# Causal attention with sixteen heads: one column-tile stretch a pair of steps, maxima at the front of each score stretch, the diagonal mask added by TensorE

## What is computed

```python
scores = jnp.einsum('bhqd,bhkd->bhqk', q, k) / math.sqrt(dk)
causal = jnp.tril(jnp.ones((S, S), dtype=bool))
scores = jnp.where(causal[None, None], scores, -jnp.inf)
attn = jax.nn.softmax(scores, axis=-1)
ctx = jnp.einsum('bhqk,bhkd->bhqd', attn, v)
```

## Time and profile before

| | |
|---|---|
| Median of 3 runs | 1840.8 us (1836.97 to 1855.38) |
| Span of the profiled execution | 1836.8 us |
| PE busy | 1737.2 us, 95% of the span |
| DVE busy | 1167.2 us, 64% |
| POOL busy | 804.4 us, 44% |
| ACT busy | 784.3 us, 43% |
| PE weight loads busy | 1010.7 us, 55% |

### The profile page before, as it was taken

How to read it: one execution, slowest core, us unless ns; L and a number is a source line. 1 busy time by engine, 2 the same in 40 slices (tenths; PEclk the granted TensorE clock), 3 DMA queues, 4 the chain that set the end, 5 groups by cost and what they waited for, 6 DMA issues and landing times. The chain is left out here.

```text
span 1836.8 us, 33962 instructions
## 1 busy us (share of the span) xinstructions
PE 1737.2 (95%) x9952; PEld 1010.7 (55%) x9952; DVE 1167.2 (64%) x2630; ACT 784.3 (43%) x1544; POOL 804.4 (44%) x434
## 2 busy tenths in 40 slices
PE   6999995789999999989999998999999996999998
PEld 5888884444444444444445444444444433677776
DVE  6667663687767767657767775776776704566564
ACT  3222221135555545545555554554555563222321
POOL 1333333335655646535655564564664672111211
PEclk9999998599999989989999998999999997999999
DMA  5556545830161161142115006116102003131221
GB/s 172 201 197 220 194 166 174 185 72 24 25 139 25 25 131 33 25 90 70 30 35 124 25 10 137 25 25 135 29 25 71 12 7 101 41 134 69 83 100 47
DMA packets 103259, 157.60 MB, mean 86 GB/s; under 512 B 10544, under 2 KB 43824, under 8 KB 100400
## 3 DMA queue, kind: packets, MB, share of 16 engines
q1 hardware_dynamic: 93296, 136.10, 27.4%
q10 hardware_dynamic: 9792, 19.40, 2.9%
HBM read 96.23 MB, written 58.72 MB: 84 GB/s over the span
## 5 line engine op out<-in xcount | busy, mean ns | idle before, releaser
L771 ACT ACTIVATE a_probs<-a_st 128x512 f32<-128x512 f32 (+3 forms) x1280 | 613.2, 536 | 543.3 <-PE a_st L661 277.7
L618 POOL TENSOR_TENSOR a_pair<-a_probs 128x1024 f32<-128x1024 f32 (+2 forms) x320 | 614.8, 1938 | 396.7 <-ACT a_probs L771 396.7
L790 DVE TENSOR_REDUCE a_part<-a_mx 128x1 f32<-128x512 f32 x768 | 507.7, 684 | 208.8 <-PE a_mx L649 206.8
L649 PE MATMUL a_mx<-a_k_stack,a_q_stack 96*128 96x512 f32 (+3 forms) x1280 | 493.5, 428 | 45.1 <-DMA a_q_stack<-qk_scratch 24.5
L661 PE MATMUL a_st<-a_q_stack,a_k_stack 98*128 98x512 f32 (+3 forms) x1280 | 447.9, 393 | 5.1 <-ACT a_probs L771 2.2
L649 PEld LDWEIGHTS a_mx<-a_k_stack,a_q_stack 96*128 96x128 f32 x1280 | 229.7, 196 | 389.5 <-DVE a_part L790 179.5
L794 DVE CUSTOM_DVE_ANT_0 a_mx<-a_mx,a_mask 128x384 f32<-128x384 f32 (+3 forms) x512 | 250.5, 498 | 140.7 <-PE a_mx L649 138.1
L661 PEld LDWEIGHTS a_st<-a_q_stack,a_k_stack 98*128 98x128 f32 x1280 | 242.8, 193 | 83.6 <-ACT a_probs L771 52.7
L217 POOL TENSOR_TENSOR p_rot<-p_mul 128x1024 f32<-128x1024 f32 x32 | 90.7, 2836 | 213.3 <-DVE p_mul L412 213.3
L675 PE MATMUL a_av<-a_probs,shared 128*32 128x512 f32 (+3 forms) x1280 | 161.7, 551 | 0.7
L675 PE MATMUL a_av<-a_probs,a_v 128*32 128x512 f32 (+3 forms) x1280 | 160.0, 546 | 0.7
(11 more groups left out here) (138 smaller groups left out, 1656.8 us busy)
## 6 DMA issues: line engine op xcount, KB each, us to landing
a_q_stack<-qk_scratch SPq DMA_DIRECT2D x96, 256.0 KB, 4.9
a_k_stack<-qk_scratch SPq DMA_DIRECT2D x21, 1024.0 KB, 13.7
qk_scratch<-p_rot_hi SPq DMA_DIRECT2D x32, 512.0 KB, 3.1
qk_scratch<-p_rot_lo SPq DMA_DIRECT2D x32, 512.0 KB, 3.9
v_scratch<-p_v_st SPq DMA_DIRECT2D x32, 256.0 KB, 6.1
ctx_scratch<-a_ctx_st SPq DMA_DIRECT2D x32, 256.0 KB, 2.4
f_ctx<-ctx_scratch SPq DMA_DIRECT2D x8, 1024.0 KB, 8.9
f_x<-in_x SPq DMA_DIRECT2D x8, 1024.0 KB, 7.8
```

What stands on the lines that cost most here:

```text
L618: pool.tensor_tensor(pair[:, p % 2, h:h + 2, q0:TT], probs[:, s % RING, h:h + 2, q0:TT], probs[:, (s + 1) % RING, h:h + 2, q0:TT], ALU.add ...
L649: pe.matmul(mx_ps[k % BANKS][:, 0:width], q_stack[0:96, t, h, qi * P:(qi + 1) * P], k_stack[par][0:96, h, c * TT:c * TT + width], start=Tr ...
L771: act.activation(probs[:, s % RING, h, q0:TT], st_ps[:, (HG * s + h) % BANKS, q0:TT], ACT.Exp, scale=SCORE_SCALE).then_inc(exp_done, 1)
L790: dve.tensor_reduce(out, mx_ps[k % BANKS][:, :], AX.X, ALU.max).then_inc(max_done, 1)
```

## The change

It does five things.

1. Work goes by pairs of steps. PE issues the eight score products of the next pair, then one column stretch that holds the values of both steps and the sums of the same pair (`values_and_sums`). ACT waits for the sums once a pair, and the ring `a_probs` has four steps.
2. The items of a pair stand among its eight scores, two ahead of the first and then about one ahead of each, none in the column stretch. The table now counts by pairs, and the counts differ by up to two from those of the two steps before.
3. On the diagonal an item gets its mask on PE: a second, bf16 product of `a_later` and `a_eye` of 128 columns into the same bank. DVE then takes a `tensor_reduce` for every item, of the item's width. The mask in SBUF, its memset and its wait go.
4. On DVE `turn_sums` stands ahead of the items of a pair, `invert` and `turn_back` behind the first and the second; `unit_max` still comes behind the items of the stretch in which a unit's items end.
5. SP's waits and the order of its copies follow the pairs.

```diff
-LAG = 2
-RING = 5
+RING = 4
+LAST_PAIR = [e // 2 for e in UNIT_END]
...
-PER_FIRST = 7
+PER_FIRST = 14
...
+    room = [width(2 * p + 2) + width(2 * p + 3) + 2 * width(2 * p) + width(2 * p + 1) + 0.5 for p in range(NPAIR)]
+    for e in LAST_PAIR:
+        room[(e + 1) % NPAIR] -= 1.0
...
-                pe.matmul(mx_ps[k % BANKS][:, 0:width], q_stack[0:96, t, h, qi * P:(qi + 1) * P],
-                          k_stack[par][0:96, h, c * TT:c * TT + width], start=True, stop=True).then_inc(item_done, 1)
+                mm = pe.matmul(mx_ps[k % BANKS][:, 0:width], q_stack[0:96, t, h, qi * P:(qi + 1) * P],
+                               k_stack[par][0:96, h, c * TT:c * TT + width], start=True, stop=c < t)
+                if c == t:
+                    mm = pe.matmul(mx_ps[k % BANKS][:, width - P:width], later[:, :], eye[:, :], start=False, stop=True)
+                mm.then_inc(item_done, 1)
...
+            def values_and_sums(g, par, p):
...
+                pe.wait_ge(exp_done, exps(g, steps[1], HG - 1))
+                if unit_first:
+                    pe.wait_ge(av_copied, 4 * g + t + START)
+                for n, (s, q) in enumerate(zip(steps, (q0, q1))):
+                    for h in range(HG):
+                        mm = pe.matmul(av_ps[h * DK:(h + 1) * DK, q:TT], vb[par][:, j + n, h * DK:(h + 1) * DK],
+                                       probs[:, s % RING, h, q:TT], start=unit_first and n == 0,
+                                       stop=unit_last and n == 1, tile_position=(0, h * DK))
+                mm.then_inc(values_done, 1)
...
+                pe.wait_ge(pair_added, 2 * (NPAIR * g + p) + 2)
+                for h in range(HG):
+                    mm = pe.matmul(sum_ps[h * DK:(h + 1) * DK, q1:TT], ones[:, :], pair[:, p % 2, h, q1:TT],
+                                   start=unit_first and q1 == q0, stop=unit_last, tile_position=(0, h * DK))
+                mm.then_inc(pair_done, 1)
...
+                for p in range(NPAIR):
+                    items = [(n, k) for n, k in items_of_pair(p, first) if not (n and last)]
                     issued = 0
+                    for i in range(2 * HG):
+                        while issued < len(items) and issued * 2 * HG <= (i + 1) * len(items):
...
+                    values_and_sums(g, par, p)
...
-                    wait_alone(dve, item_done, NITEM * g + k + 1, dve_passed)
-                    dve.tensor_tensor_reduce(out=mx_ps[k % BANKS][:, 0:width], in0=mx_ps[k % BANKS][:, 0:width],
-                                             in1=mask[:, TT - width:TT], scale=1.0, scalar=3.0 * MASKED,
-                                             op0=ALU.add, op1=ALU.max, accum_out=out).then_inc(max_done, 1)
+                width = TT if c < t else (qi + 1) * P
+                dve.wait_ge(item_done, NITEM * g + k + 1)
+                dve.tensor_reduce(part[:, h * SUB + qi, c:c + 1], mx_ps[k % BANKS][:, 0:width], AX.X,
+                                  ALU.max).then_inc(max_done, 1)
```

More of the change, by code:

```diff
@@ L77, in plan_items, with items_before, items_of_pair, units_ended_at_pair @@
 def plan_items():
[L80 to L84, removed]
+    room = [width(2 * p + 2) + width(2 * p + 3) + 2 * width(2 * p) + width(2 * p + 1) + 0.5 for p in range(NPAIR)]
+    for e in LAST_PAIR:
+        room[(e + 1) % NPAIR] -= 1.0
+    done = [sum(room[:p]) / sum(room) * NITEM for p in range(NPAIR + 1)]
     return [HEAD_START + round(d) for d in done]
 PLAN = plan_items()
[L91 to L110, removed]
+def items_before(p, first):
+    steady = PLAN[p % NPAIR] + NITEM * (p // NPAIR)
+    return min(BEFORE_FIRST + PER_FIRST * p, steady) if first else steady
+def items_of_pair(p, first):
+    return [(f // NITEM, f % NITEM) for f in range(items_before(p, first), items_before(p + 1, first))]
+def units_ended_at_pair(p, first):
+    return [(n, ITEMS[k][0]) for n, k in items_of_pair(p, first) if k in ITEM_END]
+def unit_ended_before(p, pairs):
+    e = p - pairs
+    return [(int(e < 0), t) for t in range(QT) if LAST_PAIR[t] == e % NPAIR]
 def wait_alone(eng, semaphore, value, passed):
@@ L619, in add_pairs @@
                                            probs[:, (s + 1) % RING, h:h + 2, q0:TT], ALU.add).then_inc(pair_added, 1)
-                    for ahead, t_out in unit_ended_before(s, 1):
-                        if not (ahead and first):
-                            divide(g - ahead, t_out)
+                    for before, t_out in unit_ended_before(p, 1):
+                        if not (before and first):
+                            divide(g - before, t_out)
             def divide(g, t):
@@ L700, in sums @@
                 mm.then_inc(pair_done, 1)
             def group(g, par, use, next_use, first, last):
-                for s in range(NSTEP):
-                    items = [(n, k) for n, k in items_of_step(s, first) if not (n and last)]
+                for p in range(NPAIR):
+                    items = [(n, k) for n, k in items_of_pair(p, first) if not (n and last)]
                     issued = 0
-                    add_pair = (s - LAG) % 2 == 1 and not (s < LAG and first)
-                    total = width(s + 1) + width(s) + (width(s - LAG) if add_pair else 0.0)
-                    def items_due(work):
-                        nonlocal issued
-                        while issued < len(items) and issued * total <= work * len(items) + 1e-6:
+                    for i in range(2 * HG):
+                        while issued < len(items) and issued * 2 * HG <= (i + 1) * len(items):
@@ L858, in _ @@
             group(GROUPS - 1, False, True)
-            for part_of, _, _ in PARTS:
-                part_of(GROUPS - 1, QT - 1)
+            turn_sums(GROUPS - 1, QT - 1)
+            invert(GROUPS - 1, QT - 1)
+            turn_back(GROUPS - 1, QT - 1)
 class Early:
```

164 lines of the change are left out of this document (62 added, 102 removed).

## The result

The changed kernel takes 1895.5 us (median of 4 runs, 1892.0 to 1896.5), the kernel before 1838.9 us (4 runs, 1832.3 to 1855.4). The ratio is 1.029, with a 95% interval from 1.024 to 1.034: 57 us slower. The forecast was 1930, 34 us too high. The direction was right, and so was the cause of most of the loss; the sum's +96 us was 39 too large. The profiled execution has a span of 1894.2 us.

A forecast was written before the change was run, and what follows sets the result against it. The prediction took PE to bound the attention (busy 1147 of 1172 us). Switches, masks and bursts (-15), loop turn (+4), unit_max meeting POOL (+72) and clock (+35) gave +96 on 1836.8: 1933, stated as 1930 us, range 1830 to 1975.

The forecast's parts named there:

- The switches: PE between array products and column stretches: 0.343 us lost per stretch, 320 stretches fewer, -110 us.
- The mask products: Diagonal items on PE: 512 second products at 0.125 us each, +64 us; 20 us if every weight load hid.
- The bursts: Items among scores wait for DVE behind three banks: 5.6 us a group after the change, little of the 110 left.
- its -15: Sum over all groups of switches, mask products and bank waits on PE: -15 us.
- The hand rules: Products of a group's 20 pairs timed by predecessor or bank release: 139.5 us a group before, 137.2 after.
- unit_max and POOL: CAST and subtraction behind pairs 1, 9, 11, 15 held by POOL's additions: 10.1 us a loop group, +72 us.
- the 1 us named: Sign of being right: CAST and subtraction behind pairs 1, 11 and 15 last 1 to 2.4 us each.
- The clock: Half clock on PE behind 14 waits of about 4 us, 2.5 us each: +35 us, from 0 to 70.
- That unit_max slips by: Rival: the CAST precedes POOL at pairs 1 and 11, or both instructions run beside POOL: 1826 us; chance 0.23.
- That the subtraction gets in between POOL's two instructions: Rival: only the CAST is held, DVE is free 2.3 us sooner: 1864 us; chance 0.10.
- The third: Rival: the clock falls for 10 us behind each long wait, 35 becomes 70: 1975 us; chance 0.09.
- The loop turn: At DVE's loop end PE's wait grows from 1.21 to 1.9 us, six times: +4 us.

The follow-up runs named there:

- e9: Kernel before with unit_max's three tensor_reduces (as in e3) and VectorE reducing only the last 128 columns of each item: 1822.3 us.
- e12: e7 without the 512 mask products of the items: 1710.1 us.
- e5: e1 with the mask of the diagonal items added by VectorE again instead of by a product on PE: 1796.7 us.
- e7: e1 with VectorE reducing only the last 128 columns of each item, all of PE's work kept: 1747.3 us.
- e3: Kernel before with unit_max's CAST and subtraction replaced by three small tensor_reduces of one SBUF input each: 1832.0 us.
- e1: Changed kernel with unit_max's CAST and subtraction replaced by three small tensor_reduces of one SBUF input each: 1802.3 us.
- e2_one_of_two: Changed kernel with only unit_max's CAST replaced by a tensor_reduce, the subtraction kept: 1843.1 us.

## Why the prediction was right, and where it was off

The runs part both kernels into the same layers. The columns add up by construction. Each entry but the first line's is the difference of two runs that differ in one thing; e9 and e12 differ in the whole order of work, stretches, places of the items and turn alike. The order in which layers are taken off matters too, as e5 showed for the masks.

| us | before | after | change | predicted |
|---|---|---|---|---|
| PE's own work with ACT's pace, items without mask products | 1822.3 (e9) | 1710.1 (e12) | -112 | -110 |
| mask products on PE | 0 | 37.1 (e7 - e12) | +37 | +64 |
| DVE's pace behind three banks | 9.7 (e3 - e9) | 55.0 (e1 - e7) | +45 | +31 |
| unit_max beside POOL, with the clock | 7.5 (before - e3) | 93.2 (after - e1) | +86 | +107 |
| loop turn of DVE | | | in the rows above | +4 |
| sum | 1839.5 | 1895.4 | +56 | +96 |

**The forecast.** The working gives +96, which is 1937 us on the median before of 1840.8. It was added to a span of 1836.8 instead, taken for an execution 4 us below the median, and 1933 was then rounded down; but in the runs here a time is 1.7 to 3.9 us longer than its span, so a short span says little. By this the stated time came out nearer than the working.

**The switches: right in price, and by luck so close in the sum.** Three losses of 0.095, 0.143 and 0.105 us were read from single rows, and 320 of them came to 112 us instead of 110. One stretch more cost 0.25 to 0.37 us in a pair at PE's pace. But the working had the same gain in every group, 13.7 us, and between e9 and e12 (by first exponentials) it is 16 to 18 in the groups of the loop without a loop end of PE, 10 in the first and 4 in the last. In the last, a pair without items even grew from 5.93 to 6.29 us. The very pair from which the price was read gained nothing, since ACT set its length afterwards.

**The mask products: mis-sized, the largest single miss.** The step "512 items get one: +64 us" took the price of a 512 wide product for all. It should have been kept as one end of a range: measured 37 us, and 42 in the order of before.

**The bursts: mechanism right, 14 us too small in the sum.** The prediction found that much of the gain from the switches vanishes behind the banks. Its 5.6 us for a group of the loop was met: 5.5 between e7 and e1. The +31 of the table is what its -15 leaves beside -110 and +64, and it has 1.7 us a group taken off for ACT's holds before, 14 us over eight groups, which the table's first line contains; no run separates them. Without the meeting with POOL the change is 30 us better than before (e1 against e3), not 11 (-15 and the loop's +4); the masks' 27 us too much and the bursts' 14 too little leave most of that.

**The hand rules.** They gave 139.5 us for a group before, and the trace has about 143 where the clock is full. The working named this miss, 55 us over the attention, and put it down to loop ends and clock mostly. e9 shows that 3 to 5 us of it a group are PE's own time, which the rules had too short. They had it too short for the changed order as well: without masks they give 131.5 - 64 x 0.125 = 123.5 us a group, and e12 has 126.5 to 127.4. There the mask's price, too high, hid it: e7 has 132.2 against 131.5. It did little harm, since the switches were priced from rows.

**unit_max and POOL: right in place and cause.** Behind pairs 1 and 11 PE waits 3.8 and 3.45 us, predicted 3 to 4.5. In the six groups of the loop the pair with the wait is longer than in e1_no_port by 5.1 to 6.7 us behind pair 1 (predicted 3.9 + 2.5), by 5.5 to 6.2 behind pair 11 (4.3 + 2.5) and by 1.3 behind pair 15 (1.7). Behind pair 9 nothing is lost (predicted 0.1), though CAST and subtraction take 1.07 and 1.74 us there: a hold costs only where PE has to wait for a bank behind it. In pair 15 the CAST took 0.91 us, just under the 1 us named. In pair 11 the prediction had the CAST 0.6 us behind POOL's start; it was 0.70. The Trainium skill, "SBUF — State Buffer", section "Who interferes with whom", says that a `tensor_reduce` never asks for the ports that a cast and an operation with two SBUF inputs share with GpSimd. e1_no_port agrees: reductions of the same numbers at the same places took 0.17 to 0.21 us.

**The clock: about right for each.** Taking the wait of 3.8 or 3.45 us from the loss of its pair leaves at least 1.3 to 2.9 us for the clock and what else is late, against 2.5 predicted. By first scores a group of the loop is 12.6 to 14.6 us longer than in e1_no_port, predicted 15.1, which makes 9 less over six groups; the first group is 10.9 longer (predicted 8 + 2.5), the last 5.6 (4 + 2.5). So the two traces are 98 us apart against 107 predicted. The medians are 93 apart, since the profiled e1_no_port was 5 us faster than its median. And the 7.5 us that the order before already paid were not taken off. Together that is the miss of 21. No run has the long waits without the low clock, so the split into 72 and 35 is not shown, only the sum.

**The rivals.** That unit_max slips by (1826 us) is refuted by the rows of the tile. That the subtraction gets in between POOL's two instructions is refuted as well: it starts 0.04 us behind the CAST and is held to POOL's end. The third, 10 us of low clock behind each long wait, is true of few: of the seventeen stretches of low clock between 460 and 1480 us two stand at the ends of PE's loop, and of the fifteen others eleven lasted 6.8 us and four 10.2. Behind pair 1, where both kinds occur, the pair is 6.5 to 6.7 us longer with 10.2 us and 5.1 to 6.0 with 6.8.

**The loop turn.** DVE stood for 2.3 us there in e1_no_port, and PE's wait was 0.7 us, where the working had it grow from 1.21 to 1.9. The term of +4 us had the wrong sign; it was too small to matter.

## What to carry to other kernels

A short operation is no cheap one when it shares something with a long one. Ask of each small VectorE copy, cast or two-input operation what GpSimd does at that moment, and after a change of order ask again; where the result can be had by a reduction, as here, the question goes away. And before paying TensorE time to relieve VectorE, or the other way, find out which sets the pace in the new order: here moving the same mask from VectorE to TensorE cost 42 us in one order and 6 in the other.

## What the runs showed of the hardware

- A VectorE operation of 175 ns took up to 1.88 us (CAST) and 2.30 us (subtraction) beside GpSimd's two-input addition of 2.4 us (4.66 for two). Two such in a row were held by two GpSimd instructions in a row: between the two, the waiting one went ahead (619.18), and the next was held by GpSimd's second.
- With each of the fourteen waits of 3.35 to 3.82 us behind a `unit_max` come 6.8 or 10.2 us at the 1.2 GHz level; the 10.2 us begin while PE still waits. In e2_one_of_two 3.4 or 6.8 us followed 9 of 13 waits of 1.15 to 1.5 us. In e1_no_port, with waits up to 0.8 us, the clock stayed full from 380 to 1480 us except behind the two ends of PE's loop, where PE stood for 3.1 and 3.2 us; but in e2_one_of_two it fell once, for 10.2 us from 385.2 on, behind a wait of 0.68.
- Holds of 0.1 to 0.3 us for each product cost 55 us and appear as 14.6 us of idle time. The mean duration of an item's row (422 ns against 406 with short maxima) hardly shows them; the waits of its weight loads do (97.3 us against 8.8).
- Column stretches between scores gave ACT time to catch up: with three of them a pair without items took 5.93 us, with one 6.29.
